# A graph attention layer on one core: the residual branch leaves the first stage and is made beside the attention units

## The reference

```python
h = maximum(layernorm(x), 0)
hh = (h @ W.T).reshape(n, H, D)
s_src = einsum('nhd,hd->nh', hh, a_src);  s_dst = einsum('nhd,hd->nh', hh, a_dst)
attn = s_src[:, None, :] + s_dst[None, :, :] + adj[:, :, None] * We[:, 0] + be
attn = softmax(leaky_relu(where(adj > 0, attn, -inf), 0.2), axis=1)
out = x + einsum('ijh,jhd->ihd', attn, hh) + h @ Wr.T + br
```

## Time and profile before

| | us |
|---|---|
| median of 3 runs | 2684.43 |
| lowest, highest | 2674.48, 2684.55 |
| the profiled execution's own time | 2684.95 |
| its span (first to last instruction) | 2683.3 |

### The profile page before, as it was taken

One profiled execution on the slowest core, in us unless ns is written; L12 is line 12 of the kernel. 1 busy time (PEld: TensorE's weight loads), 2 busy tenths in 40 slices (PEclk: granted clock), 3 DMA queues, 4 the chain that ended last, 5 costly groups with the idle time before them and its releaser, 6 DMA issues.

```text
span 2683.3 us, 27007 instructions
## 1 busy us (share of the span) xinstructions
PE 1235.0 (46%) x5305; PEld 934.2 (35%) x5306; DVE 2132.3 (79%) x4852; ACT 1246.5 (46%) x4898; POOL 1485.7 (55%) x1666
## 2 busy tenths in 40 slices
PE   6990022503334367446424524533341453518885
PEld 4660022402324245334322512422241342416664
DVE  3448959998998898999889988988997841259992
ACT  2320030221245498667546546444542655826662
POOL 5772656756675777777777476277347437710000
PEclk9995556757666676666666666666665666759998
DMA  3665656686676877877777677678668614477660
GB/s 114 195 228 191 216 131 195 167 249 178 179 226 192 225 240 225 245 229 243 229 224 239 199 233 222 183 231 233 208 193 234 200 39 100 95 225 173 157 156 3
DMA packets 226527, 512.79 MB, mean 191 GB/s; under 512 B 98280, under 2 KB 116400, under 8 KB 224208
## 3 DMA queue, kind: packets, MB, share of 16 engines
q1 hardware_dynamic: 151280, 319.60, 37.2%
q0 software_dynamic: 74960, 191.61, 28.1%
q10 hardware_dynamic: 144, 0.13, 0.0%
HBM read 475.19 MB, written 36.03 MB: 191 GB/s over the span
## 4 chain that ended last, share of the span: by engine, by line
DMA 56%; issue 18%; PE 10%; DVE 6%; POOL 6%; ACT 2%; SPq 1%; POOLq 0%; DVEq 0%; ACTq 0%; PEldq 0%
DMA adj_sb<-in_adj_dram 40%; DMA arena<-table,arena 8%; DMA arena<-table,own 6%; POOL arena L493 5%; PE banks L1058 2%; PE banks L1052 2%; ACT arena L947 1%; PE banks L1101 1%; DVE work L619 1%; PE banks L1079 1%; DVE work L615 1%; PE banks L1055 1%; PE banks L1154 1%; PE banks L1144 1%; DMA out_dram<-w_all,arena 1%
## 5 line engine op out<-in xcount | busy, mean ns | idle before, releaser
L493 POOL DMA_INDIRECT arena<-table,arena x943 | 972.6, 1031 | 354.5 <-issue 231.2
L1079 PE MATMUL banks<-arena,ident 128*128 128x256 f32 x1268 | 426.9, 513 | 1142.1 <-DVE arena L755 1142.1
L947 ACT ACTIVATE arena<-arena,prob 128x32 f32<-128x32 f32 x4024 | 859.5, 306 | 2.1
L1079 PEld LDWEIGHTS banks<-arena,ident 128*128 128x128 f32 x1268 | 332.6, 268 | 1234.8 <-issue 984.6
L615 DVE MAX8 work<-adj_sb 128x8 f32<-128x184 f32 (+51 forms) x624 | 580.9, 1005 | 116.0 <-DMA adj_sb<-in_adj_dram 115.5
L619 DVE FIND_INDEX8 work<-work,adj_sb 128x8 uint32<-128x184 f32 (+51 forms) x624 | 618.6, 1013 | 0.0
L942 ACT ACTIVATE prob<-pre 128x104 f32<-128x104 f32 (+26 forms) x63 | 20.3, 322 | 965.6 <-DVE pre L739 965.6
L1085 PE MATMUL banks<-arena,ident 128*128 128x256 f32 x1006 | 312.6, 442 | 106.3 <-ACT arena L947 106.2
L493 POOL DMA_INDIRECT arena<-table,own x194 | 202.2, 1042 | 157.4 <-DMA arena<-table,own 55.6
L1085 PEld LDWEIGHTS banks<-arena,ident 128*128 128x128 f32 x1006 | 197.3, 212 | 209.0 <-ACT arena L947 188.5
L932 ACT ACTIVATE pre<-arena,we_all 128x13 f32<-128x13 f32 (+23 forms) x480 | 146.5, 400 | 80.1 <-DMA arena<-lists 80.1
(11 more groups left out here) (140 smaller groups left out, 1789.2 us busy)
## 6 DMA issues: line engine op xcount, KB each, us to landing
adj_sb<-in_adj_dram SPq DMA_DIRECT2D x504, 512.0 KB, 4.0
arena<-dst_rows SPq DMA_DIRECT2D x16, 2048.0 KB, 8.5
arena<-table,arena POOLq DMA_INDIRECT x943, 3.5
table<-arena POOLq DMA_DIRECT2D x32, 264.0 KB, 2.9
arena<-in_x_dram SPq DMA_DIRECT2D x32, 256.0 KB, 3.0
resid<-arena POOLq DMA_DIRECT2D x32, 256.0 KB, 2.6
out_dram<-arena POOLq DMA_DIRECT2D x32, 256.0 KB, 2.8
work<-table SPq DMA_DIRECT2D x8, 1024.0 KB, 10.9
```

The source lines that it names most:

```text
L493: pool.indirect_dma_start(gath[:, un.slot(k), :], None, table[:, :], bass.IndirectOffsetOnAxis(ap=rec[:, k, 0:1], axis=0), bounds_check=N ...
L947: last = s.activation(g, g, ACT.Copy, scale=prob[:, b, k * H + h:k * H + h + 1])
L1079: last = m.matmul(ps_sum[:, u % 2, :], ident[:, :], gath[:, un.slot(k), 0:HD], start=(k == 0), stop=False)
```

## The change

The dst scores are no longer computed twice; the small columns are kept (`sd_all`) and turned on PE once at the end of the prelude. The product with `Wr` leaves the prelude. Instead POOL writes the normalised rows after the relu to a DRAM buffer `normed`, and each of the 64 tiles gets a step `residual(t)` later: ACT loads the tile's normalised rows and its x, PE makes four matmuls (two with `Wr`, one that adds `br` and one that adds `x`, both through the identity), ACT copies the sum out of PSUM and writes it to `out` and `resid`. 13 tiles come ahead of the first unit, then one per unit; ACT copies it one unit after PE made it. To make room the gather ring has 81 slots in place of 86; the output buffers and a few others move.

```diff
-GSLOTS = 86
+GSLOTS = 81
+RES_FIRST = 13
...
+    normed = nc.dram_tensor("normed", (UNITS, P, 2 * IN), F32, kind="Internal").ap()
...
-        hnT = part(2 * 2 * IN).rearrange("p (u b n) -> p u b n", u=2, b=2)
+        hnT = part(4 * 2 * IN).rearrange("p (u b n) -> p u b n", u=4, b=2)
...
-            with pool.Fori(0, UNITS // 2) as i:
-                for q in range(2):
-                    u = 2 * i + q
-                    pool.wait_ge(S["hd_copied"], u + 1)
-                    pool.dma_start(by_unit(table[PAD:PAD + N, :], u), hd_sb[:, q, :, 0:ROW]).then_inc(S[f"hd_out{q}"], 16)
-                    pool.wait_ge(S["dst_copied"], u + 1)
-                    pool.dma_start(dst_rows[:, bass.ts(u, 2 * P)].rearrange("h (b p) -> h b p", b=2),
-                                   dst_sb[0:H, q, :, :]).then_inc(S[f"dst_out{q}"], 16)
...
-                    nc.gpsimd.tensor_tensor(rt_sb[:, q, :, :], rt_sb[:, q, :, :],
-                                            br_all[:, :].unsqueeze(1).to_broadcast([P, 2, HD]), ALU.add
-                                            ).then_inc(S["br_added"], 1)
...
-                    pool.dma_start(by_unit(resid, u), rt_sb[:, q, :, :]).then_inc(S[f"res_out{q}"], 16)
-                    pool.dma_start(by_unit(out, u), rt_sb[:, q, :, :]).then_inc(S[f"res_out{q}"], 16)
+            def keep_normed(u, q):
+                pool.wait_ge(S["hnT_done"], u + 1)
+                pool.dma_start(normed[bass.ts(u, 1), :, :].rearrange("a p n -> (a p) n"),
+                               hnT[:, q, :, :].rearrange("p b n -> p (b n)")).then_inc(S[f"normed_out{q}"], 16)
+
+            def keep_table(u, q):
+                pool.wait_ge(S["hd_copied"], u + 1)
+                pool.dma_start(by_unit(table[PAD:PAD + N, :], u), hd_sb[:, q % 2, :, 0:ROW]).then_inc(S[f"hd_out{q % 2}"], 16)
...
@@ DVE, add_biases
+                v.tensor_copy(sd_all[:, bass.ts(u, 2), :], hd_sb[:, q % 2, :, HD:ROW])
                 v.tensor_tensor(s_all[:, bass.ts(u, 2), :], hd_sb[:, q % 2, :, ROW:ROW + H],
...
-                v.tensor_tensor(rt_sb[:, q % 2, :, :], ps_res[:, q % 2, :, :], x_sb[:, q, :, :], ALU.add
-                                ).then_inc(S["res_done"], 1)
@@ ACT
-                s.activation(dst_sb[0:H, q % 2, :, :], ps_dst[0:H, q % 2, :, :], ACT.Copy).then_inc(S["dst_copied"], 1)
...
+            def load_residual(t):
+                b = t % 3
+                if t >= 3:
+                    act.wait_ge(S[f"res_out{b}"], 32 * (t // 3))
+                act.dma_start(hx_sb[b][:, 0:IN], normed[t // 2, :, t % 2 * IN:(t % 2 + 1) * IN]).then_inc(S[f"hx_in{b}"], 16)
+                act.dma_start(hx_sb[b][:, IN:2 * IN], x[bass.ts(t, P), :]).then_inc(S[f"hx_in{b}"], 16)
+            def residual(t):
+                b = t % 3
+                act.wait_ge(S["res_ps"], t + 1)
+                s.activation(hx_sb[b][:, IN:2 * IN], ps_res[:, t % 2, :], ACT.Copy).then_inc(S["res_done"], 1)
+                act.wait_ge(S["res_done"], t + 1)
+                act.dma_start(out[bass.ts(t, P), :], hx_sb[b][:, IN:2 * IN]).then_inc(S[f"res_out{b}"], 16)
+                act.dma_start(resid[bass.ts(t, P), :], hx_sb[b][:, IN:2 * IN]).then_inc(S[f"res_out{b}"], 16)
+                if t + 2 < TILES:
+                    load_residual(t + 2)
...
+            load_residual(0)
+            load_residual(1)
+            for t in range(RES_FIRST):
+                residual(t)
             prepare(units[0])
             for un in units:
                 if un.u + 1 < len(units):
                     prepare(units[un.u + 1])
                 exps(un)
+                if un.u and RES_FIRST + un.u - 1 < TILES:
+                    residual(RES_FIRST + un.u - 1)
@@ PE, maps
-                        m.matmul(ps_hd[:, q, b, :], rows, w_all[:, c, 0:272], start=(c == 0), stop=(c == 1))
-                        m.matmul(ps_dst[0:H, q, b, :], w_all[:, c, HD:ROW], rows, start=(c == 0), stop=(c == 1))
-                        last = m.matmul(ps_res[:, q, b, :], rows, w_all[:, c, 272:528], start=(c == 0), stop=(c == 1))
+                        last = m.matmul(ps_hd[:, q, b, :], rows, w_all[:, c, 0:272], start=(c == 0), stop=(c == 1))
...
+            def residual(t):
+                b = t % 3
+                pe.wait_ge(S[f"hx_in{b}"], 32 * (t // 3 + 1))
+                if t >= 2:
+                    pe.wait_ge(S["res_done"], t - 1)
+                for c in range(2):
+                    m.matmul(ps_res[:, t % 2, :], hx_sb[b][:, c * P:(c + 1) * P], w_all[:, c, 272:528], start=(c == 0),
+                             stop=False)
+                m.matmul(ps_res[:, t % 2, :], ident[:, :], br_all[:, :], start=False, stop=False)
+                m.matmul(ps_res[:, t % 2, :], ident[:, :], hx_sb[b][:, IN:2 * IN], start=False, stop=True)
...
+            for t in range(RES_FIRST):
+                residual(t)
             for un in units:
...
                 tile_sums(un)
+                if RES_FIRST + un.u < TILES:
+                    residual(RES_FIRST + un.u)
```

97 lines of the change are left out of this document (64 added, 33 removed).

## The result

| | us |
|---|---|
| the changed kernel, median of 4 runs | 2734.82 (2731.24 to 2741.20) |
| the kernel before beside it, median of 4 runs | 2681.87 (2674.48 to 2684.55) |
| ratio, with its 95% interval | 1.0199 (1.0175 to 1.0222) |
| the profiled executions, before and changed | 2684.95 and 2741.20 (spans 2683.3 and 2739.6) |

What follows compares the result with a forecast made beforehand. PE alone was taken to bound the prelude, and the latency of adj pieces loaded one behind the other the unit stage. -61 + 8 + 2 + 29 = -22 us from 2684.95 gave 2663 us, range 2635 to 2702.

Steps and rivals of the forecast that it cites:

- the sum: Whole program: -61 prelude, +8 gather ring, +2 engines, +29 DMA in the unit stage, together -22 us.
- DMA and engines together: Unit stage: residual transfers delaying adj pieces, 29 us, and added work of PE and ACT, 2 us.
- the prelude: Prelude: a pair of tiles takes 3.5 us in place of 5.46, DVE with ACT setting the pace; gain 61 us.
- R1: Prelude rival: PE's clock falls to 1.2 GHz, 4.6 us a pair, gain only 30, total 2694 us; chance 0.14.
- R2: Prelude rival: x lands in 5 us, so landings bound, 4.1 us a pair, gain 44, total 2680 us; chance 0.10.
- the 13 first tiles: Before the first unit: 13 residual tiles, 3.3 us each, 43 us in all, covered by waiting; cost 0.
- the ring: First units: five fewer gather slots put five gathers behind POOL's wait for PE, delaying unit 3; cost 8 us.
- done before ACT's first edge term is wanted: Sign for the profile after: the 13 residual tiles finish before ACT's first edge term is wanted; no size given.
- the measured quarter: Unit stage: 1.23 us of gather work delays an adj piece by 0.31; basis for pricing residual transfers at 29 us.
- R3: Unit stage rival: adj chain pays each residual burst in full, 1.6 us a tile, 67 us; total 2701; chance 0.16.
- The marks I had set: Unit stage signs: adj waits about 3.8 us each, first to last find some 39 us longer, wrong if over 60.
- Engines: 2 us: Unit stage: PE's four matmuls, ACT's copy and issues per unit mostly fit free time; cost 2 us.

## Why the prediction was wrong

The forecast was -22 us, the two traces differ by +56.3, so 78 us are to be placed. 46.6 of them are a term that the sum didn't have (the end part), and 31 are the adj-bound stretch, 61.8 where DMA and engines together were put at 31. What is left cancels.

**Right: the prelude.** Forecast -61, measured -65.1. The loop of DVE with ACT sets the pace, 3.45 to 3.7 us by the rows above against 3.5; PE 72% busy against 70; clock 1.00; landings 3.1 us, 12.25 MB and 6.06 MB at 41.7% and 29.9%, a DMA share of 0.72 against 0.71. That this share came out so near is luck: x took 1.0 us a pair of all engines and the writes 1.4, where I had 0.77 and 1.72. The first scan begins at 144.25 us (forecast 148); the last x load came 59 us earlier (forecast 58), and from there it took 18.6 us and not 21. R1 and R2 fall: the clock did not go down with PE's pauses, and DVE waited 5.3 us for x. R1's price stood on a reading that the profile does not give: its record of the clock begins at 40.6 us, so that PE ran at 1.2 GHz at 27 us was read from the duration alone (2.02 us for four L1052, twice 0.92). The copy of the score columns took 0.17 to 0.18 as taken.

**Right in cost: the 13 first tiles and the ring.** The tiles cost nothing, as forecast, but not as I said: they took ACT from 145 to 212 us, 67 us in place of 43 (a copy every 4.1 us, behind a first load that landed late under the flood of adj), and my sign "done before ACT's first edge term is wanted" failed by 24 us. ACT's wait of 88 us for DVE covered it. POOL's first ring wait was 16.43 (forecast some 16). The ring of 81 in the kernel before alone cost 9 us on the way to the eleventh scan, where I took 8. The way it goes was not the one I gave (unit 3's gathers) but the deal of the lists behind POOL's gathers, ACT's edge term, DVE. The changed kernel lost 14.8 us there; some 5 of them are not the ring's. 3.6 lie ahead of the exp of unit 0, where the first gathers land later beside the residual tiles (DVE waits 32.8 us for them in place of 29.4); what the rest is stays open.

**Failed: "the measured quarter".** The step that failed is the price of the residual's transfers on the adj chain, "0.7 us a tile, nearer the lower end: 29 us". The runs show 54.5 us for the transfers alone (1.3 us a tile, 81% of the 1.6 that I had as the whole of it), and the stretch grew by 61.8 in the profiled executions; three kernels with the old chain and no residual beside it had it in 1212.3, 1213.0 and 1217.3 us, so a few of the other 7 are spread. It is R3's mechanism, for which I had given 0.16 and a price of 67. The quarter came from comparing pieces with gathers beside them and pieces without. That compares two states of a program, in which more differs than the gathers; why it came out so low no run here shows. An edit gives the slope, and the slope was three times the quarter; of the next half megabyte it was 62%, still over twice the quarter, so the full price of R3 is an upper bound too. The rule that I had named against the change, DMAs of all issuing engines run on the same sixteen engines (the Trainium skill, DMA: Bandwidth & Descriptors, Issuing engines are not separate DMA queues), pointed the right way, and I let an indirect number outweigh it. The marks I had set said so: SP's wait 3.91 us a piece (R3: 3.9), first to last scan longer by 2006.1 - 1931.5 = 74.6, over the 60 that I had called wrong.

**Missing: the end part.** 46.6 of the 56.3 us are ACT's loop over the flags at a dear place of its code. Put in my own terms: the sum went from the unit stage straight to the total, with nothing for the end, and gave no reason for it. I had costed ACT's added instructions by their time alone, not by what they push back. R3's forecast of +16 with these 47 would be +63, near the measured 56. Without the end part the changed kernel is 0.3% slower, within what I had called no change and within the range, though not the gain that I forecast.

**Engines: 2 us.** PE's matmuls and ACT's copies beside the units: 1215.9 us with them and 1220.5 without, so nothing that can be seen, against 2 forecast; ACT's issues are not in this, as they went with the transfers.

## What to carry to other kernels

Where transfers are issued one behind the other's landing, take the waiting engine's time per transfer and the count as the price list. Here traffic beside the chain was paid at 78% of its own packets' time, and the next as much at 62%. Before moving traffic beside such a chain, put a second transfer in flight. A difference between stretches of one trace is no slope; for the cost of added bytes, run a kernel with added bytes, and until then keep the full engine time as the upper bound, and the forecast near it, where there is no slack. Any edit that adds instructions to an engine can move a later loop of that engine to a place where each round fetches code; look at the end of the program and at the instruction queues' packets.

## What the runs showed of the hardware

- One loop of about 265 instructions on ACT took 1.27 us a round or 8.35 to 8.68, by its place in ACT's code alone; in the slow case 38 packets of 8 KB passed on the instruction queue in 71 us.
- One adj piece of 512 KB in flight beside gathers: 3.8 us to land; two: 4.9 us each, 1.1 us more for twice the pieces.
- Another 0.52 MB a tile on ACT's queue raised the wait for a piece from 3.71 to 3.92 us, another 0.52 MB of stores to 4.04.
- A DMA issue took 0.35 to 0.5 us of ACT's queue, and a residual tile ahead of the units 4.1 to 4.4 us.
- PE, busy 57.87 of 80 us in the prelude, kept the granted clock of 1.00 (2.4 GHz).
